# Causal-window attention between two gated feed-forward phases, one core: values on pairs of query blocks, unrolled feed-forward phases with the layer norm on GpSimd, transposes three steps behind

## The reference

```python
x = x + 0.5 * ffn(layernorm(x))          # phase A, first half
x = x + attn(layernorm(x))               # phase A, second half, and the attention
x = x + 0.5 * ffn(layernorm(x))          # phase D
# x: 4 x 1024 x 128, float32
# ffn:  silu(x @ wg.T) * (x @ wu.T) @ wd.T, hidden size 384, integer weights / 127
# attn: h = silu(x @ W1.T + b1) @ W2.T + b2;  q, k, v = h @ Wg.T + bg, 16 heads of 64
#       dots masked where j >= i + 64, softmax, times v, then @ Wo.T + bo
```

## Time and profile before

| what | value |
|---|---|
| median of 3 runs | 1634.21 us (1634.13 to 1634.35) |
| the profiled execution's own time | 1628.43 us |
| its span | 1626.6 us |
| PE busy | 1439.0 us, 88% of the span |
| DVE, ACT, POOL busy | 970.6, 776.3, 990.7 us |
| DMA queue's share of 16 engines | 5.9% |
| chain that ended last, by engine | PE 55%, issue 17%, DVE 13%, POOL 7%, ACT 6% |

### The profile page before, as it was taken

The page is one execution under the profiler, slowest core; times in us unless marked ns, Lnnn a source line. Parts: engine busy times, 40 slices in busy tenths (PEclk is TensorE's granted clock), DMA queues, the critical chain, the costliest instruction groups (busy, mean ns, idle before and its releaser), DMA issues.

```text
span 1626.6 us, 38540 instructions
## 1 busy us (share of the span) xinstructions
PE 1439.0 (88%) x13330; PEld 1113.7 (68%) x13330; DVE 970.6 (60%) x1886; ACT 776.3 (48%) x1827; POOL 990.7 (61%) x592
## 2 busy tenths in 40 slices
PE   4767999999999999999999999999999999998676
PEld 3543777777777777777777777777777777777566
DVE  5653666666666666566666656666666656665444
ACT  2323555555555455554555555555555455454332
POOL 2231767677666667666676766677666666667410
PEclk9995999999999999999999999999999999999978
DMA  3100000000000000000000000000000000000000
GB/s 96 36 0 18 19 19 19 18 18 18 18 18 18 13 5 18 18 18 18 18 18 18 18 18 18 18 18 18 18 18 18 18 1 17 18 0 1 1 26 26
DMA packets 30571, 29.42 MB, mean 18 GB/s; under 512 B 6993, under 2 KB 25298, under 8 KB 30546
## 3 DMA queue, kind: packets, MB, share of 16 engines
q1 hardware_dynamic: 30546, 29.09, 5.9%
HBM read 8.07 MB, written 2.10 MB: 6 GB/s over the span
## 4 chain that ended last, share of the span: by engine, by line
PE 55%; issue 17%; DVE 13%; POOL 7%; ACT 6%; DVEq 1%; DMA 1%; ACTq 0%; POOLq 0%; SPq 0%
PE banks L773 16%; PE banks L754 15%; PE banks L789 8%; PE banks L719 6%; POOL probs L324 6%; ACT probs L389 5%; DVE probst L549 4%; DVE negmax L537 4%; PE banks L655 4%; PE banks L742 2%; PE banks L723 2%; DVE hidden L492 1%; PE banks L734 1%; POOL rstd_ln L295 1%; DVE xn_ln L478 1%
## 5 line engine op out<-in xcount | busy, mean ns | idle before, releaser
L324 POOL TENSOR_SCALAR probs<-probs,recips 128x704 f32<-128x704 f32 (+7 forms) x512 | 947.6, 1864 | 452.5 <-DVE recips L542 452.5
L537 DVE TENSOR_REDUCE negmax<-banks 128x1 f32<-128x704 f32 (+7 forms) x512 | 392.6, 808 | 129.8 <-PE banks L754 129.8
L773 PE MATMUL banks<-ident,probs 128*128 128x128 f32 x2752 | 391.4, 281 | 43.2 <-DVE probst L549 22.6
L397 ACT ACTIVATE probst<-banks 128x512 f32<-128x512 f32 (+1 forms) x320 | 177.4, 555 | 516.2 <-PE banks L773 516.2
L389 ACT ACTIVATE probs<-banks,negmax 128x704 f32<-128x704 f32 (+7 forms) x512 | 397.2, 785 | 44.5 <-DVE negmax L537 44.5
L773 PEld LDWEIGHTS banks<-ident,probs 128*128 128x128 f32 x2752 | 293.2, 141 | 130.3 <-issue 69.3
L549 DVE COPY probst<-banks 128x512 f32<-128x512 f32 (+1 forms) x416 | 276.6, 665 | 171.8 <-PE banks L773 169.8
L789 PE MATMUL banks<-probst,vs 128*64 128x128 f32 x5504 | 357.0, 277 | 0.8 <-ACT probst L397 0.8
L789 PEld LDWEIGHTS banks<-probst,vs 128*64 128x64 f32 x5504 | 295.3, 137 | 37.6 <-issue 22.5
L754 PE MATMUL banks<-kt,qt 64*128 64x512 f32 (+4 forms) x2496 | 298.3, 365 | 3.1 <-issue 3.1
L754 PEld LDWEIGHTS banks<-kt,qt 64*128 64x128 f32 x2496 | 206.0, 186 | 50.5 <-issue 5.8
(11 more groups left out here) (58 smaller groups left out, 881.1 us busy)
## 6 DMA issues: line engine op xcount, KB each, us to landing
hslot<-h_sb SPq DMA_DIRECT2D x32, 512.0 KB, 3.2
wslot<-in_wqkvt SPq DMA_DIRECT2D x32, 128.0 KB, 3.0
wslot<-wq_sb SPq DMA_DIRECT2D x32, 64.0 KB, 2.6
y<-xres SPq DMA_DIRECT2D x8, 256.0 KB, 2.3
wo_sb<-in_wot SPq DMA_DIRECT2D x1, 512.0 KB
wq_sb<-in_wqkvt SPq DMA_DIRECT2D x1, 512.0 KB
bslot<-bqk_sb SPq DMA_DIRECT2D x32, 1.0 KB, 1.9
iload<-in_wgatet SPq DMA_DIRECT2D x1, 192.0 KB, 2.4
```

The lines of the kernel that those rows point to most:

```text
L324: nc.gpsimd.tensor_scalar(here, here, recips[:, c, h:h + 1], None, ALU.mult).then_inc(normed.sem, 1)
L397: nc.scalar.activation(probst[c % 2][:, 4 * g:4 * g + w, :].rearrange("p t q -> p (t q)"), banks[:, TRANSPOSED[g % 2], 0:w * P], ACT.Copy) ...
L537: nc.vector.tensor_reduce(negmax[:, c, h:h + 1], src, AX.X, ALU.max, negate=True).then_inc(maxed.sem, 1)
L773: last = nc.tensor.transpose(banks[:, TRANSPOSED[g % 2], (t - 4 * g) * P:(t - 4 * g + 1) * P], probs[c, h][:, kb * P:(kb + 1) * P], ident[:])
```

## The change

The attention's steps get `T_LAG, PV_LAG = 3, 5`. `attend` works on pairs of query blocks (0,1), (2,3), (4,5), (6,7), in steps 5, 7, 1 and 3, with 256 columns where both blocks have the key block. ACT takes the even transpose groups and DVE the odd ones. `k1`, `q1`, `v0`, `v1` of a turn are projected in the turn's own steps 0, 2, 4 and 5; `k0` and `q0` of the next turn both in step 6, behind `o0`. Before turn 0 only `k0` and `q0` are projected, in banks 5 and 6. The feed-forward phases are unrolled, with `xn`, `xth` and `hidden` in two buffers and statistics in two or three; `down` comes one iteration after `gate_up`, and the ln1 normalisation moves from DVE to POOL. The first 512 tokens are loaded first, by a DMA of their own. At the end `o1`, `o2` and `o3` of the last turn follow the last attend.

```diff
-    T_LAG, PV_LAG = 2, 3
+    T_LAG, PV_LAG = 3, 5
...
-    JOBS = {0: ["k0"], 1: ["o2", "q0"], 2: ["k1"], 3: ["o3", "q1"], 4: ["v0"], 5: ["o0"], 6: ["v1"], 7: ["o1"]}
+
+    ATTEND_AT = {5: 0, 7: 1, 1: 2, 3: 3}
+
+    JOBS = {0: ["o1", "k1"], 1: [], 2: ["o2", "q1"], 3: [], 4: ["o3", "v0"], 5: ["v1"], 6: ["o0", "k0", "q0"], 7: []}
+    FIRST = (("k0", 5), ("q0", 6))
```

On PE, the product with the values and the order within a step (a `v` or `k`/`q` job first waits, through `misc_read`, for the job before it in `JOBS`):

```diff
-                for kb in range(blocks[c]):
+                for kb in range(blocks[c1]):
+                    q = slice(0 if kb < blocks[c0] else P, 2 * P)
                     for h in range(2):
-                        last = mm(banks[half(h), ATTEND, 0:P], vs[r][:, kb, half(h)], probst[c % 2][:, 2 * kb + h, :],
-                                  start=(kb == 0), stop=(kb == blocks[c] - 1), skip_group_check=True)
+                        last = mm(banks[half(h), ATTEND, q], vs[r][:, kb, half(h)], probst[p % 2][:, 2 * kb + h, q],
+                                  start=(kb == 0), stop=(kb == blocks[c1] - 1), skip_group_check=True)
...
                 score(c, i, r)
                 if turning:
                     turns_of(tc, ti, (0, 1))
-                for job in JOBS[c]:
-                    if job[0] == "o":
-                        do(job)
+                for job in JOBS[c][:1]:
+                    do(job)
                 if attending:
-                    attend(ac, ai, r if c >= PV_LAG else 1 - r)
+                    attend(ATTEND_AT[c], *((i, r) if c >= PV_LAG else (i - 1, 1 - r)))
+                for job in JOBS[c][1:2]:
+                    do(job)
                 if turning:
                     turns_of(tc, ti, (2, 3))
-                for job in JOBS[c]:
-                    if job[0] != "o":
-                        do(job)
+                for job in JOBS[c][2:]:
+                    do(job)
```

On ACT the step becomes:

```diff
+                turning = carry or c >= T_LAG
+                if turning:
+                    take(tc, 0, ti)
+                exps(c, i)
+                if turning and groups[tc] > 2:
+                    take(tc, 2, ti)
+                if c in ATTEND_AT and (carry or c >= PV_LAG):
+                    attention_out(ATTEND_AT[c], i if c >= PV_LAG else i - 1)
+                for job in JOBS[c]:
+                    if job[0] in "kq" and runs(job, carry, more):
+                        queries_keys(job, job_turn(job, i), 1 - r if job_turn(job, 0) else r)
```

On DVE (`evict` is the addition, the copy of values or the low part, by the job's kind):

```diff
                 row_max(c, i)
-                if turning:
-                    take(tc, 0, ti)
-                for job in JOBS[c]:
-                    if job[0] == "o" and (carry or job in ("o0", "o1")):
-                        add_output(job, job_turn(job, c, i))
-                if turning and groups[tc] > 2:
-                    take(tc, 2, ti)
+                if turning and groups[tc] > 1:
+                    take(tc, 1, ti)
+                for job in JOBS[c][:1]:
+                    evict(job, i, r, carry, more)
+                if turning and groups[tc] > 3:
+                    take(tc, 3, ti)
                 invert(c, i)
...
+                for job in JOBS[c][1:]:
+                    evict(job, i, r, carry, more)
```

The feed-forward phases on PE:

```diff
+            def feed_forward(ph):
+                transposed(ph, "ln1", 0)
...
+                for t in range(CHUNKS + 3):
+                    if t < CHUNKS:
+                        gate_up(ph, t)
...
+                    if ph is pa and 0 <= t - 3 < CHUNKS:
+                        outer(t - 3)
+                    if t + 1 < CHUNKS:
+                        transposed(ph, "ln1", t + 1)
+                    if 0 <= t - 1 < CHUNKS:
+                        down(ph, t - 1)
+                    elif ph is pa and 0 <= t - 2 < CHUNKS:
+                        transposed(pa, "ln2", t - 2)
+                        for name, bank in FIRST:
+                            project(name, 0, 0, bank)
+                    if ph is pa and 0 <= t - 2 < CHUNKS:
+                        inner(t - 2)
```

On DVE:

```diff
+                for t in range(CHUNKS + 2):
+                    if t < CHUNKS:
+                        gate(ph, t)
+                    if ph is pa and 0 <= t - 2 < CHUNKS:
+                        layernorm2(t - 2)
+                    if t + 1 < CHUNKS:
+                        low(ph, t + 1)
+                    if t + 3 < CHUNKS:
+                        statistics(ph, "ln1", t + 3)
+                    if 0 <= t - 1 < CHUNKS:
+                        residual(ph, t - 1)
+                        if ph is pa:
+                            statistics(pa, "ln2", t - 1)
```

And on POOL, which takes over the ln1 normalisation:

```diff
+            def layernorm(ph, t):
+                done(pool, ph.rstd["ln1"], "r", t)
+                done(pool, ph.tr["ln1"], "t", t - 2)
+                pool.sem_inc(idle, 1)
+                for k in range(CT):
+                    nc.gpsimd.tensor_scalar(xn["ln1"][t % 2][:, k, :], xres[:, t * CH + k * D:t * CH + (k + 1) * D], mv["ln1"][t % 3][:, k, 0:1],
+                                            rstd["ln1"][t % 3][:, k:k + 1], ALU.subtract, ALU.mult).then_inc(ph.norm["ln1"].sem, 1)
```

More of the change, by code:

```diff
@@ L297, in add_bias @@
-            def add_bias(turn, at):
-                pool.wait_ge(pa.norm["ln2"].sem, pa.norm["ln2"].after("n", turn))
-                here = xres[:, bass.ds(at, CT * D)].rearrange("p (k d) -> p k d", d=D)
-                nc.gpsimd.tensor_tensor(here, here, bo_all[:].unsqueeze(1).to_broadcast([P, CT, P]), ALU.add).then_inc(pa.biased.sem, 1)
-            rstd_of(pa, "ln1", 0)
-            rstd_of(pa, "ln1", 1)
[L305 to L308, removed]
@@ new lines, in silus, with inner @@
+            def silus(ph, t):
+                for j in range(HB):
+                    done(act, ph.gu, f"g{j}", t)
+                    done(act, ph.hid, f"h{j}", t - 1)
+                    nc.scalar.activation(gated[:, j, :], banks[:, 1 + j, :], ACT.Silu, scale=FS).then_inc(ph.silu.sem, 1)
+            def inner(t):
+                done(act, pa.m1, "m", t)
+                done(act, pa.m2, "m", t - 1)
+                nc.scalar.activation(y1[:], banks[:, T_BANK["ln2"], :], ACT.Silu, bias=b1_sb[:]).then_inc(pa.y1.sem, 1)
@@ L574, in add_output, with evict @@
                 nc.vector.tensor_tensor(here, banks[:, MISC, 0:2 * P], here, ALU.add).then_inc(wo_added.sem, 1)
+            def evict(job, i, r, carry, more):
+                if not runs(job, carry, more):
+                    return
+                if job[0] == "o":
+                    if not carry:
+                        done(dve, pa.biased, "b", CHUNKS - 1)
+                    add_output(job, job_turn(job, i))
+                elif job[0] == "v":
+                    values(job, i, r)
+                else:
+                    queries_keys_low(job, job_turn(job, i), 1 - r if job_turn(job, 0) else r)
             def step(c, i, r, carry=True, more=True):
@@ L636, in transposed, with gate_up @@
                 for k in range(CT):
[L637 to L641 removed]
+                    last = nc.tensor.transpose(banks[:, T_BANK[ln], k * P:(k + 1) * P], src[:, k, :], ident[:])
+                last.then_inc(ph.tr[ln].sem, 1)
+            def gate_up(ph, t):
+                done(pe, ph.xlo, "l", t)
@@ L650, in down @@
-            def down(t, turn):
-                pe.wait_ge(t.hid.sem, t.hid.after(f"h{HB - 1}", turn))
-                pe.wait_ge(t.x1.sem, t.x1.before("x", turn))
+                        done(pe, ph.hid, f"h{j - HB}", t - 1)
+                    mm(banks[:, 1 + j, :], wff[:, j, :], xth[t % 2][:, 0, :], start=True, stop=False)
+                    mm(banks[:, 1 + j, :], wff[:, j, :], xth[t % 2][:, 1, :], start=False, stop=True).then_inc(ph.gu.sem, 1)
+            def down(ph, t):
+                done(pe, ph.hid, f"h{HB - 1}", t)
+                done(pe, ph.x1, "x", t - 1)
```

574 lines of the change are left out of this document (252 added, 322 removed).

## The result

The changed kernel takes **1698.97 us** (median of 4 runs, 1694.96 to 1701.95) beside 1634.17 us for the kernel before on the same chip. The ratio is 1.0401, 95% interval 1.0374 to 1.0429: slower by 4%. The forecast had the direction and not the size: 1664 us, +30, where +65 came. The range, 1570 to 1705, holds it. The profiled execution took 1694.96 us, its span is 1693.1 us.

The account below looks back on a forecast made before the run. A turn was taken as bound by PE's order, the softmax chain or the one job bank, feed-forward phases by engines waiting for each other. -43 - 39 + 78 + 1.5 + 33 = +30.5 gave 1659, rescaled 1664 us; range 1570 to 1705.

Parts of the forecast that it names:

- Phase A: First feed-forward phase and its projections: pipelined chunk 9.1 us instead of 12.2, attention starts at 104 us, -43 us.
- Phase D: Last feed-forward phase: 6.1 us a chunk, 96.1 us becomes about 57, -39 us.
- The turn walked: Attention turn, summed step by step from row distances: 45.5 us, +2.5 a turn, +78 us in all.
- The serial chain of step 6: Step 6: o0, k0 and q0 share one bank, PE idles 1.9 us twice, 9.4 us from scores to scores.
- The clock: PE's granted clock falls at step 6's idle spells, 2.15 us a turn; half of the turns taken, +33 us.
- I take half of the turns: Attention turns: of bounds from nothing to 2.15 us in each turn (+67), half was taken, +33 us.
- Drain: After the last turn: last attend of 16 blocks, not 8, three output jobs one behind another, less earlier statistics; +1.5 us.
- Values on pairs: Attend: half as many matmuls and weight loads save nothing, as the columns alone fill the time; priced at nothing.
- Clock falls in every turn: Rival for the attention: 1631 + 67 = 1698 us, up to 1715 if step 7's transposes are slow too; chance 0.14.
- Turn nearly as before: Rival: shorter job bank chain or PE's pieces closing up, a turn of 43 to 44.5 us, 1553 to 1600; chance 0.20.

Follow-up runs that it names:

- both waits filled: Changed kernel with sixteen matmuls that nobody reads before k0's wait and sixteen before q0's in step 6; 1627.89 us, ratio 0.9968.
- one wait filled: Changed kernel with sixteen matmuls that nobody reads before only one wait of step 6: k0's 1671.04 us, q0's 1638.27 us (one run each).
- the mended form: Changed kernel with k0's wait in step 6 filled, q0 moved to step 7 right behind the scores and its evictions moved too; 1572.62 us, ratio 0.9624.
- the combination with 12 fillers: Changed kernel's feed-forward phases around the attention turn of the kernel before, 12 matmuls that nobody reads ahead of turn 0; 1553.33 us, ratio 0.9516.

## Why the prediction was right in direction and wrong in size

**Phase A** (-43): measured -49.1. The chunk takes 8.07 us, not 9.1, with PE busy all of it, below even the bound of 8.6. Probably the ends counted in the 8.86 of the earlier trace rows overlap their successors once the pieces stand back to back (argued). DVE is busy 6.73 us of it.

**Phase D** (-39): measured -38.9; the chunk takes 5.92 us, 5.9 in the working. Busy time of a chunk of phase A and one of phase D in the changed kernel, columns as in the earlier trace rows:

```profile
46.13:54.20 8.07, 8.07 (x51) 6.52 (x49) 6.73 (x26) 3.92 (x7) 6.99 (x10) 1.00 0.23 73
...
1660.00:1665.92 5.92, 5.92 (x43) 5.32 (x42) 4.43 (x14) 2.17 (x5) 4.40 (x7) 1.00 0.14 44
```

**The turn walked** (4.6, 5.65, 5.1, 5.5, 4.9, 4.8, 9.4, 5.6): measured, scores to scores, 4.68, 5.76, 5.13, 5.56, 4.91, 4.76, 10.20, 6.82. Six steps are within 0.11 us. Step 7 is longer by 1.22, its scores being slow by 1.28. k0 starts 4.91 us after the scores of step 6 (forecast 4.80 to 4.91), q0 at 8.08 (forecast 8.2, though the terms given for it add up to 7.9 to 8.0). With both waits filled, where the clock is out of it, the middle turn is 45.57 us, against 45.5 walked. The serial chain of step 6, +2.5 a turn, is right in place and size: of the 149.1 us that the attention up to its last scores grew, 67.9 are the clock's and 81.2 are left for the 78 forecast.

**The clock** (+33) is the term that was mis-sized. The price of one fall was right, 2.15 us forecast and 2.19 measured. "I take half of the turns" was wrong: it falls in all 31, so the term is +68, and its error of 35 us is that of the whole forecast (the other terms missed by -6, +3 and +4, which cancel). The half came from the chunk of phase A that kept 1.00 with idle time of like sum. That was the wrong row: its 3.3 us are three waits, of which these are the first and the last.

```profile
72.49 0.66 PE L637 MATMUL banks<-ident,xn_ln 128*128 128x128 f32 x4 [1.49 <-DVE xn_ln L478]
...
76.60 2.95 PE L655 MATMUL banks<-wdn,hidden 128*128 128x128 f32 x24 [1.13 <-DVE hidden L492]
```

Step 6 has two waits of 1.87 and 1.83 us with 1.3 us of work between. The row with a wait of 2.11 us in one piece had the clock fall. That the length of the single wait is what tells the rows apart is argued. The page cited in the prediction, the Trainium skill's "TensorE: Matmul & The Clock Gate" (HAM oscillation), describes bursts of about 2 us between waits of 3 to 5 us, longer than those of step 6; what it warns of, every round starting cold, is what the trace shows here, but that it gave every turn was read into it. Nor does it follow from all turns being alike that the clock falls in all or in none: the runs with one wait filled had it in 16 and in 12 turns of 31.

**Drain** (+1.5): measured +5.3. Three output jobs stand behind one another, 1.23 us each, where the kernel before has two, and two products of pairs with 13 and 16 blocks' columns, 3.03 and 3.67 us, stand where single blocks did. The forecast paid, in sum, for little more than the longer last product.

**Values on pairs** at nothing: right for PE's time. The run without pairs shows it piece by piece, though its total alone would have said the opposite, because its loop stalls.

**The rivals.** "Clock falls in every turn", 1698 us, given 0.14, is what happened. "Turn nearly as before" is what the mended form reaches (1572), but not the change as written. None of the rivals had the place of the loop in it; in the changed kernel it did no harm (16 packets), so it did not bear on the forecast, only on the attempt to take the change apart.

**What is left of the change.** The new phases with the old turn give 1553.3 us, the new phases with the mended new turn 1572.6. By their stages the new turn starts 11.3 us earlier (99.55 for 110.81, as only k0 and q0 are projected ahead of turn 0 and the other four within it), and loses 22.0 us over 31 turns and 8.5 in the last turn and drain. The gain is all in the feed-forward phases; the attention half of the change brings none, mended or not. The best kernel found is the combination with 12 fillers, 4.8% faster than the kernel before and, by the two ratios, 8.5% faster than the change.

## What to carry to other kernels

Follow a moved job on every engine that reads its bank, not only on the one that computes it: two jobs through one bank cost a full round of evictions, and moving the second without its evictions only moves the wait. Waits of PE that repeat in every turn should be priced with the clock by the row whose idle time lies in one piece as theirs does, and the case of a fall in every turn deserves its full weight; half-filling them with cheap matmuls is a quick test, and sometimes a cure. When a loop gets slower though its code did not change, read the instruction queue's packets and the idle time that is put down to issue before you explain anything by the work in it.

## What the runs showed of the hardware

- **Place of a loop in the instruction stream.** The same loop (1,576 matmuls and weight loads of TensorE in a pass, 1,701 instructions in the trace) ran 15 passes from 15 to 19 packets of 16 KB in all, or took 142 to 145 packets. Then 14 passes began with idle PE, 3.4 to 3.5 us on average and 4.0 at most, in one form 1.7 us more a pass, and the clock fell to 0.50 behind it. The cost was 92 to 106 us in all. 24 instructions ahead of the loop decided it. A loop of 1,704 matmuls and weight loads stalled in the same way at the one place where it was tried. The Trainium skill ("Runtime: NRT & Kernel Launch", Instruction fetch mechanics) gives TensorE room for 2,048 instructions, refilled in blocks of 256; the packets of 16 KB agree, but both loops that stalled are shorter than that room by the trace's count. The same section says that a taken branch out of a window of two blocks always has to fetch; the trace contradicts it, as a loop of more than six such blocks repeats here without a fetch.
- **What keeps the clock.** Two waits of 1.87 and 1.83 us, 1.3 us of work between, brought it down in 31 turns of 31; the same places with 0.97 and 0.94 us left idle, in none; with only the first wait half filled it fell in 16, with only the second in 12 (one run each).
- **A bf16 matmul of 128 columns** with the same operands took 0.056 us from start to start in a row of sixteen (1.06 us for sixteen, the modelled end of the last included).
